# Graph sum layer: the own-row half of the mixing made in the stage that normalises, kept in DRAM with its bias, and a reordered score chain in attention

## The chip, the cores and the metric

The kernel runs on one core of one Trainium2 chip, as one launch. The metric is device time in microseconds (us) from start to end of an execution, the median of several runs. TensorE (PE), VectorE (DVE), ScalarE (ACT), GpSimd (POOL) and SyncE (SP) each run their own instruction stream in order and meet at semaphores.

## The reference

`x` is 6250 nodes by 256 features in float32, with 100000 edges sorted by target node. Four residual steps follow each other; the change touches the first (attention, three layers) and the third (graph sum):

```python
x = x + gat3(layernorm(x))                  # three attention layers, segment softmax over edges
x = x + moe_gelu(layernorm(x))              # 8 experts, 2 a node, and a shared one
e = layernorm(x)                            # "embeddings" of the graph sum
ego  = e @ W1.T + b1                        # own-row product
nb   = segment_sum(edge_val * e[src], dst)  # neighbours
side = (nb + nb * e) @ W2.T + b2
out  = leaky_relu(ego + side, 0.2)
x = x + out / max(norm(out), 1e-12)
x = x + moe_relu(layernorm(x))              # 4 experts, 2 a node, and a shared one
```

## The kernel before

Nodes lie in NT = 49 tiles of 128 rows; blocks of UT = 7 tiles make NB = 7 blocks. Edges lie in 28 groups (NG) of 28 columns (GB) of 128 edges. Code is written by hand for each engine; stages follow each other with a barrier between, so a stage's time is that of its latest engine, the last DMA that it waits for included. In combine and mix_end every loop over tiles is unrolled.

**attention_pass** (three times, line 872 on). POOL gathers the rows of a group's 28 columns by 28 indirect DMAs (L956) into one half of a two-half buffer. DVE waits for a group's rows, copies the scores to `terms` (L1085), and runs a chain of small operations, in turns with PE's transposes, which finds each edge's segment maximum: `differ` (L1027 to L1032, six operations that compare the open node tile's peak; ACT makes `scale` of them, L1151), `shut`, `x`, scans `up` and `top` (L1090 to L1096), `scale_sums` (L1038), after PE's `prow` the scans `fore` and `back` (L1103), `scale_old` (L1044), after PE's `pcar` the copy `carry` (L1109) and the scans again, `merge`, and after `paid` the weighing of the rows (`weigh`, L1058) with one-hot matrices (`hots`, L1064) for PE's sum over edges (L1217). `differ` waits for `kept`, ACT's copy of the last finished sum.

**combine** (line 2062 on) adds the expert outputs, `routed`, to X and normalises to `rows`/`emb`. SP loads the blocks of `routed` (896 KB each) into a ring of R = 3 (L2081), waiting only for `added`, so up to three blocks ahead. DVE runs `vary(i)` (add L2106, statistics) and `norm(i)` (L2121) in the order vary(0), vary(1), norm(0), vary(2), norm(1), ..., vary(6), norm(5), norm(6). ACT takes the square root of a block's variances and issues the store of each normalised block to the DRAM table `emb` (L2093). PE and POOL have nothing to do.

**loads** and **add_into** follow: SP loads the mixing weights `w` (W1T and W2T), two bias rows and the router's weights, and DVE adds the biases to `gbias`. Then **edge_pass** gathers rows of `emb` and sums them.

**mix_end** (line 1555 on), tile by tile: SP loads a block of `emb`; DVE makes `fin` = (1 + e) * nb (L1590); PE transposes e and fin (4 of 128x128, L1615); ACT copies them to `xt`; PE multiplies with W1T and W2T (4 products of 128x128 by 128x256, each float32 product is 2 recorded instructions, L1623); DVE adds `gbias` (L1598) and applies the leaky slope (L1600); ACT squares. In DVE's order tile t's `fin` stands ahead of tile t-2's last two operations; in PE's, tile t's transposes ahead of tile t-1's products.

Of the kernel before, what the change touches and what calls it, by code (L numbers as in the profile page):

```python
# [35 lines left out]
ALU = mybir.AluOpType  # L36
# [3 lines left out]
P = 128  # L40
# [831 lines left out]
def attention_pass(nc, kit, c, table, accs):  # L872
# [7 lines left out]
    with kit.stage() as st:  # L880
# [55 lines left out]
        with nc.Block() as block:  # L936
# [41 lines left out]
            def _(dve):  # L978
# [95 lines left out]
                with dve.Fori(0, NG // 2) as i:  # L1074
                    for h in range(2):
# [6 lines left out]
                        for k, n in enumerate((HALF, GB - HALF)):  # L1082
# [4 lines left out]

                        dve.wait_ge(kept, m + low + 2)
                        differ(before)
                        linked(v.tensor_copy(shut[:, :], flat(c.penT[:, 1, ds(m), :])))  # L1090
# [7 lines left out]

                        dve.wait_ge(scaled, m + 1)
                        scale_sums(before)  # L1100
                        dve.wait_ge(rowed, m + 1)
# [3 lines left out]
                                             ALU.add, ALU.max).then_inc(rkept, 1)  # L1105

                        scale_old()
                        dve.wait_ge(carried, m + 3)
# [446 lines left out]
def mix_end(nc, kit, c, acc, table, outs):  # L1555


    with kit.stage() as st:
        sb, ps, sem = st.sb, st.ps, st.sem
        fin = sb("fin", [P, UT, D])  # L1560
        xt = sb("xt", [P, UT, 4, P])
        pT = [ps(f"pT{k}", [P, 4, P]) for k in range(2)]
        pH = [ps(f"pH{k}", [P, D]) for k in range(2)]
# [3 lines left out]
        prod, hkept, made, squared = sem("prod"), sem("hkept"), sem("made"), sem("squared")  # L1567
        emb_in = sem("emb_in")

        with nc.Block() as block:  # L1570
            @block.sync
            def _(sp):
                for i in range(NB):
                    sp.dma_start(outs["sbuf"][:, i * UT:(i + 1) * UT, :],
                                 table[i * UT * P:(i + 1) * UT * P, :].rearrange("(k p) d -> p k d", p=P)
                                 ).then_inc(emb_in, 16)
                    sp.wait_ge(emb_in, (i + 1) * 16)

            @block.vector
            def _(dve):  # L1580
                v = nc.vector
                dve.sem_inc(hkept, UT)
                dve.sem_inc(made, UT)
                for t in range(NT + 2):
                    if t < NT:
                        k = t % UT
                        if not k:
                            dve.wait_ge(emb_in, (t // UT + 1) * 16)
                        dve.wait_ge(turned, t + 1)
                        v.scalar_tensor_tensor(out=fin[:, k, :], in0=outs["sbuf"][:, t, :], scalar=1.0,  # L1590
                                               in1=acc(slice(t, t + 1)).rearrange("p o d -> p (o d)"),
                                               op0=ALU.add, op1=ALU.mult).then_inc(fin_made, 1)
                    if t > 1:
                        m = t - 2
                        dve.wait_ge(prod, m + 1)
                        if m:
                            dve.wait_ge(made, UT + m)
                        v.tensor_tensor(junk[:, :], pH[m % 2][:, :], c.gbias[:, :], ALU.add).then_inc(hkept, 1)  # L1598
                        dve.wait_ge(hkept, UT + m + 1)
                        v.scalar_tensor_tensor(out=outs["sbuf"][:, m, :], in0=junk[:, :], scalar=SLOPE,  # L1600
                                               in1=junk[:, :], op0=ALU.mult, op1=ALU.max).then_inc(made, 1)

            @block.tensor
            def _(pe):
                pe.sem_inc(turned, UT)
                for t in range(NT + 1):
                    k = t % UT
                    if t < NT:
                        pe.wait_ge(fin_made, t + 1)
                        if t > 1:  # L1610
                            pe.wait_ge(kept, UT + t - 1)
                        for f in range(4):
                            from_ = outs["sbuf"][:, t, :] if f < 2 else fin[:, k, :]
                            at = f % 2 * P
                            ins = nc.tensor.transpose(pT[t % 2][:, f, :], from_[:, at:at + P], c.ident[:, :])  # L1615
                        ins.then_inc(turned, 1)
                    if t:
                        m = t - 1
                        pe.wait_ge(kept, UT + m + 1)
                        if m > 1:  # L1620
                            pe.wait_ge(hkept, UT + m - 1)
                        for f in range(4):
                            ins = nc.tensor.matmul(pH[m % 2][:, :], xt[:, m % UT, f, :], outs["w"][:, f, :],  # L1623
                                                   start=(f == 0), stop=(f == 3))
                        ins.then_inc(prod, 1)
# [172 lines left out]
def experts_gelu(nc, kit, c, a, rows, slot_i, gates, group_i, slots_in, X, hT, room):  # L1798
# [3 lines left out]
    with kit.stage() as st:  # L1802
# [6 lines left out]
        xt = sb("xt", [P, 2, GS])  # L1809
        ys = sb("ys", [P, 2, D])  # L1810
        SLOTS = (MAXG + 1) * 2
# [249 lines left out]

def combine(nc, kit, c, X, emb, table):


    R = 3
    with kit.stage() as st:
        sb, sem = st.sb, st.sem
        routed = sb("routed", [P, R, UT, D])
        stats = sb("stats", [P, UT, 6])
# [3 lines left out]
        own, added, varied, rooted = sem("own"), sem("added"), sem("varied"), sem("rooted")  # L2073
        normed, stored = sem("normed"), sem("stored")
        with nc.Block() as block:
            @block.sync
            def _(sp):
                for i in range(NB):
                    if i >= R:
# [3 lines left out]
                                 ).then_inc(loaded[i % R], 16)  # L2083

            @block.scalar
            def _(act):
                for i in range(NB):
                    act.wait_ge(varied, i + 2)
                    nc.scalar.activation(std[:, i % 2, :], mv[:, i % 2, :, 1], ACT.Sqrt, bias=eps[:, :]
                                         ).then_inc(rooted, 1)  # L2090

                    act.wait_ge(normed, (i + 1) * UT)
                    act.dma_start(table[i * UT * P:(i + 1) * UT * P, :].rearrange("(k p) d -> p k d", p=P),  # L2093
                                  emb[:, i * UT:(i + 1) * UT, :]).then_inc(stored, 16)
                act.wait_ge(stored, 16 * NB)

# [228 lines left out]
def program(nc, a, out):  # L2325
# [13 lines left out]
    c.slots_in = slots_in  # L2339
    c.slot_of = dram("slot_of", [(MAXG + 1) * GS, 2])  # L2340
    c.routed = dram("routed", [NP + P, D])
    table = [dram(f"table{k}", [NP, RW]) for k in range(2)]
    emb = dram("emb", [NP, D])

    with kit.stage() as whole:
# [37 lines left out]
        with kit.stage() as rest:  # L2383
            xT = rest.sb("xT", [P, 2, NP])
            gate = rest.sb("gate", [P, NT, E1])
            gw, gb = rest.sb("gw", [P, 2, E1]), rest.sb("gb", [P, 1, E1])
            with kit.stage() as st:

                with kit.stage() as moe:
# [5 lines left out]
                    wr = moe.sb("wr", [P, 2, E0])  # L2395
                    loads(nc, kit, [(wr[:, :, :], a["L0_ffn_Wr"].rearrange("(k p) e -> p k e", p=P))])
                    with kit.stage() as route:
# [7 lines left out]
                    experts_gelu(nc, kit, c, a, rows, slot_i, (w1, w2), group_i, slots_in, X, hT, xT[:, 1, :])  # L2405
                    combine(nc, kit, c, X, rows, emb)
                sumsq = st.sb("sumsq", [P, NT])
                w = st.sb("w", [P, 4, D])
                c.gbias = st.sb("gbias", [P, D])
                b = st.sb("b", [P, D])  # L2410
                loads(nc, kit, [
                    (w[:, 0:2, :], a["W1T"].rearrange("(k p) n -> p k n", p=P)),
                    (w[:, 2:4, :], a["W2T"].rearrange("(k p) n -> p k n", p=P)),
                    (c.gbias[:, :], a["L1_gnn_b1"].rearrange("(o n) -> o n", o=1).to_broadcast([P, D])),
                    (b[:, :], a["L1_gnn_b2"].rearrange("(o n) -> o n", o=1).to_broadcast([P, D])),
                    (gw[:, :, :], a["L1_ffn_gW"].rearrange("(k p) e -> p k e", p=P)),
                    (gb[:, 0, :], a["L1_ffn_gb"].rearrange("e o -> o e").to_broadcast([P, E1]))])
                add_into(nc, kit, c.gbias[:, :], b[:, :])

                sums = xT[:, :, :].rearrange("p k n -> p (k n)").rearrange("p (t d) -> p t d", d=D)  # L2420
# [10 lines left out]
            experts_relu(nc, kit, c, a, xT, gate, X, out)  # L2431


def add_into(nc, kit, to, ap):
    with kit.stage() as st:
        done = st.sem("done")
        with nc.Block() as block:
            @block.vector
            def _(dve):
                nc.vector.tensor_tensor(to, to, ap, ALU.add).then_inc(done, 1)  # L2440

# [50 lines left out]
```

## Time and profile before

| what | value |
|---|---|
| median of the runs | 6542.59 us |
| the profiled execution's own time | 6540.51 us |
| its span, first to last instruction | 6538.9 us |
| mean granted TensorE clock | 0.819 of 2.4 GHz |
| busy share: PE, POOL, DVE, ACT | 66%, 56%, 51%, 13% |

The profiled execution lies 2.1 us under the median; 1.6 us of it lie outside its span. No engine is busy all the way: the stages have different limits, and busy shares are averages over them.

### The profile page before, as it was taken

How to read it: one execution, taken by the hardware profiler on the slowest of the kernel's cores; microseconds unless marked ns; L12 is line 12 of the kernel's file. 1: busy time of each engine (PE TensorE's matmuls, PEld its weight loads, DVE VectorE, ACT ScalarE, POOL GpSimd, SP SyncE). 2: the span in 40 equal slices, each digit the busy share in tenths (PEclk: the TensorE clock that was granted, in tenths of full speed). 3: DMA queues.
4: the chain of work that ended last, by engine and by line, in shares of the span. 5: the costliest groups of instructions: out<-in, count | busy, mean ns of one | idle time of the engine just before them, and what ended most of it. 6: DMA issues, size and time to landing. Idle time of an engine off the chain costs nothing. (4 is left out here: it accounts for less than half of the span.)

```text
span 6538.9 us, 91130 instructions
## 1 busy us (share of the span) xinstructions
PE 4292.3 (66%) x16953; PEld 3195.3 (49%) x16954; DVE 3314.1 (51%) x7793; ACT 826.7 (13%) x2019; POOL 3662.1 (56%) x3758
## 2 busy tenths in 40 slices
PE   1455667644656665455667369999992556666879
PEld 1333444433434443333444258888882444444745
DVE  7355666665566666566666731111114444444655
ACT  0200000020000002000000123322220000000322
POOL 3577777657777764777777047222222777775000
PEclk9777778876778887677888569999996777888889
DMA  5443333334333333433333233133334333333011
GB/s 174 123 113 106 106 106 106 89 110 120 106 106 106 106 95 99 124 106 106 106 106 100 84 123 88 37 66 58 60 51 117 105 105 105 105 105 96 23 49 43
DMA packets 495005, 627.74 MB, mean 96 GB/s; under 512 B 260172, under 2 KB 376904, under 8 KB 493256
## 3 DMA queue, kind: packets, MB, share of 16 engines
q0 software_dynamic: 191568, 486.53, 27.8%
q1 hardware_dynamic: 293816, 132.89, 7.6%
q10 hardware_dynamic: 9552, 7.61, 0.4%
q14 instruction: 52, 0.43, 0.0%
q8 instruction: 17, 0.28, 0.0%
HBM read 531.35 MB, written 95.78 MB: 96 GB/s over the span
## 5 line engine op out<-in xcount | busy, mean ns | idle before, releaser
L956 POOL DMA_INDIRECT rows<-table,ix x2352 | 2259.3, 961 | 741.2 <-issue 682.6
L1217 PE MATMUL acc<-rows,hot 128*128 x5856 | 1621.5, 435 | 228.0 <-DVE hot L1064 174.6
L1217 PEld LDWEIGHTS acc<-rows,hot 128*128 128x128 f32 x5856 | 1164.5, 211 | 641.4 <-issue 425.2
L1263 POOL DMA_INDIRECT rows<-emb,ix x784 | 742.0, 946 | 320.7 <-issue 229.0
L1064 DVE TENSOR_TENSOR hot<-lanes,drel 128x256 f32<-128x256 f32 x1464 | 610.2, 422 | 572.2 <-PE acc L1217 569.6
L1385 PE MATMUL acc<-rows,hot 128*128 x1952 | 582.6, 461 | 321.4 <-DVE hot L1306 308.0
L1058 DVE TENSOR_TENSOR rows<-rows,pw 128x1024 f32<-128x1024 f32 x588 | 711.6, 1210 | 0.0
L1385 PEld LDWEIGHTS acc<-rows,hot 128*128 128x128 f32 x1952 | 430.9, 232 | 456.4 <-issue 381.2
L1955 PE MATMUL p<-xt,w 128*128 128x256 f32 x2496 | 554.4, 380 | 25.4 <-DVE xt L2011 25.4
L1966 PE MATMUL p<-w,xT 128*128 128x256 f32 x2496 | 551.4, 379 | 0.0
L1955 PEld LDWEIGHTS p<-xt,w 128*128 128x128 f32 x2496 | 476.2, 191 | 90.7 <-issue 25.5
L1966 PEld LDWEIGHTS p<-w,xT 128*128 128x128 f32 x2496 | 474.2, 190 | 64.5
L1887 POOL DMA_INDIRECT routed<-ys,to_row x106 | 165.6, 1563 | 553.6 <-DVE ys L2052 340.0
L1985 ACT ACTIVATE xT<-p,b 128x256 f32<-128x256 f32 x624 | 290.2, 473 | 575.1 <-PE p L1955 572.2
L1158 ACT ACTIVATE accs<-acc x228 | 89.0, 390 | 2063.6 <-PE acc L1220 2063.6
L1306 DVE TENSOR_TENSOR hot<-lanes,drel 128x256 f32<-128x256 f32 x488 | 200.4, 422 | 217.4 <-PE acc L1385 216.3
L457 POOL DMA_INDIRECT spread<-logit,first_edge x147 | 176.1, 1198 | 225.7 <-ACT logit L1536 154.1
L2011 DVE STREAM_TRANSPOSE xt<-xg 128x512 f32<-128x512 f32 x79 | 56.2, 711 | 462.4 <-PE p L1955 445.6
L1182 PE MATMUL pS<-ident,terms 128*112 128x128 f32 x84 | 30.7, 365 | 390.3 <-DVE terms L1085 373.0
L1085 DVE COPY terms<-rows 128x112 f32<-128x112 f32 x84 | 22.2, 264 | 454.4 <-DMA rows<-table,ix 373.2
L1300 DVE TENSOR_TENSOR rows<-rows,wps 128x1024 f32<-128x1024 f32 x196 | 237.4, 1211 | 6.7 <-DMA rows<-emb,ix 6.7
L1182 PEld LDWEIGHTS pS<-ident,terms 128*112 128x112 f32 x84 | 12.7, 151 | 403.8 <-issue 403.8
(405 smaller groups left out, 4372.9 us busy)
## 6 DMA issues: line engine op xcount, KB each, us to landing
rows<-table,ix POOLq DMA_INDIRECT x2352, 2.8
xg<-slots_in SPq DMA_DIRECT2D x632, 32.0 KB
table<-hs SPq DMA_DIRECT2D x147, 130.0 KB, 2.0
own_row<-table SPq DMA_DIRECT2D x21, 896.0 KB, 11.2
slots_in<-zsp SPq DMA_DIRECT2D x9, 1664.0 KB
xin<-in_x POOLq DMA_DIRECT2D x14, 896.0 KB, 5.7
rows<-emb,ix POOLq DMA_INDIRECT x784, 2.7
w<-in_W1all POOLq DMA_DIRECT2D x9, 1024.0 KB, 7.4
```

The lines of the kernel that those rows point to most:

```text
L457: return pool.indirect_dma_start(c.spread, bass.IndirectOffsetOnAxis(ap=c.first_edge[:, t:t + 1], axis=0), c.logit[:, t, H:2 * H], None, b ...
L956: pool.indirect_dma_start(rows[:, h * GB + k, 0:RW], None, table, bass.IndirectOffsetOnAxis(ap=ix[:, h, k:k + 1], axis=0)).then_inc(landed ...
L1058: v.tensor_tensor(r, r, w.to_broadcast([P, W, H, HD]), ALU.mult).then_inc(weighed, 1)
L1064: v.tensor_tensor(hot[j][:, :, :], lanes[:, :, :].to_broadcast([P, 2, P]), c.drel[:, ds(q * W + j * 2, 2)].rearrange("p (k o) -> p k o", o ...
L1217: ins = nc.tensor.matmul(A, hot[j][:, k, :], four[:, j * 2 + k, :], start=False, stop=False, skip_group_check=True)
L1263: pool.indirect_dma_start(rows[:, h * GB + k, 0:D], None, table, bass.IndirectOffsetOnAxis(ap=ix[:, h, k:k + 1], axis=0)).then_inc(landed[ ...
L1300: v.tensor_tensor(r, r, w.to_broadcast([P, W, D]), ALU.mult).then_inc(weighed, 1)
L1306: v.tensor_tensor(hot[j][:, :, :], lanes[:, :, :].to_broadcast([P, 2, P]), c.drel[:, ds(q * W + j * 2, 2)].rearrange("p (k o) -> p k o", o ...
L1385: ins = nc.tensor.matmul(A, hot[j][:, k, :], four[:, j * 2 + k, :], start=False, stop=False, skip_group_check=True)
L1955: ins = nc.tensor.matmul(p1[f % 4][:, :], w1[b][:, k, f * P:(f + 1) * P], xt[:, k, :], start=(k == 0), stop=(k == 1))
L1966: ins = nc.tensor.matmul(p2[t][:, :], hT[:, f, t * P:(t + 1) * P], w2[b][:, f, :], start=(f == 0), stop=(f == FT0 - 1))
L1985: nc.scalar.activation(hT[:, f, :], p1[f % 4][:, :], ACT.Gelu, bias=b1[b][:, f:f + 1]).then_inc(bent, 1)
```

## The change

In **combine**, SP first loads W1T and the two bias rows. As each tile is normalised, PE transposes it and multiplies it with W1T, ACT copies both the transposes and the product out of PSUM, POOL adds the joined bias and, per block, issues the store of the 896 KB of `ego` to a new DRAM tensor. The store of the normalised block moves from ACT's queue to SP's. The buffer of `routed` lies in `xT`, which is free then. In **mix_end** the 2 transposes of e and the 2 products with W1T go; SP loads each block of `ego` behind that of `emb`, and DVE adds `ego` where it added `gbias`. The stage that loaded the weights and the one that added the biases go; W2T and the router's weights are loaded in the `loads` ahead of the experts (3 DMAs more there). `ys` of the experts lies in a spare part of `xT`. In **attention_pass** DVE's chain is reordered, and a group's first `hots` is moved ahead of the wait for `paid`.

```diff
@@ combine
+        def store(eng, i):
+            eng.wait_ge(normed, (i + 1) * UT)
+            eng.dma_start(table[...], emb[:, i * UT:(i + 1) * UT, :]).then_inc(stored, 16)
             def _(sp):
+                sp.dma_start(w[:, :, :], a["W1T"].rearrange("(k p) n -> p k n", p=P)).then_inc(fetched, 16)
+                for k, name in enumerate(("L1_gnn_b1", "L1_gnn_b2")):
+                    sp.dma_start(bias[:, k, :], a[name]...to_broadcast([P, D])).then_inc(fetched, 16)
                 for i in range(NB):
                     if i >= R:
                         sp.wait_ge(added, i - R + 1)
                     sp.dma_start(routed[:, i % R, :, :], ...).then_inc(loaded[i % R], 16)
+                    if i:
+                        store(sp, i - 1)
+                store(sp, NB - 1)
+                sp.wait_ge(stored, 16 * NB)
+            def _(pe):
+                for t in range(NT + 1):
+                    if t < NT:
+                        pe.wait_ge(normed, t + 1)
+                        if t > 1:
+                            pe.wait_ge(kept, t - 1)
+                        for f in range(2):
+                            ins = nc.tensor.transpose(pT[t % 2][:, f, :], emb[:, t, f * P:(f + 1) * P], c.ident[:, :])
+                        ins.then_inc(turned, 1)
+                    if t:
+                        m = t - 1
+                        pe.wait_ge(kept, m + 1)
+                        if m > 1:
+                            pe.wait_ge(copied, m - 1)
+                        for f in range(2):
+                            ins = nc.tensor.matmul(pH[m % 2][:, :], xt[:, m % 2, f, :], w[:, f, :], ...)
+                        ins.then_inc(prod, 1)
+            def _(pool):
...
+                for t in range(NT):
+                    pool.wait_ge(copied, t + 1)
+                    nc.gpsimd.tensor_tensor(row, row, bias[:, 0, :], ALU.add).then_inc(egos, 1)
+                    if k == UT - 1:
+                        pool.wait_ge(egos, t + 1)
+                        pool.dma_start(c.ego[i * UT * P:(i + 1) * UT * P, :]..., ego[:, i % 2, :, :])
+                for k in range(2):
+                    pool.wait_ge(ego_out[k], (NB + 1 - k) // 2 * 16)
             def _(act):
+                def take(m):
+                    i = m // UT
+                    if not m % UT and i > 1:
+                        act.wait_ge(ego_out[i % 2], i // 2 * 16)
+                    act.wait_ge(prod, m + 1)
+                    nc.scalar.activation(ego[:, i % 2, m % UT, :], pH[m % 2][:, :], ACT.Copy).then_inc(copied, 1)
-                for i in range(NB):
-                    act.wait_ge(varied, i + 2)
-                    ... Sqrt ...
-                    act.wait_ge(normed, (i + 1) * UT)
-                    act.dma_start(table[...], emb[...]).then_inc(stored, 16)
+                root(0)
+                for i in range(NB):
+                    if i < NB - 1:
+                        root(i + 1)
+                    for t in range(i * UT, (i + 1) * UT):
+                        act.wait_ge(turned, t + 1)
+                        nc.scalar.activation(xt[:, t % 2, :, :], pT[t % 2][:, :, :], ACT.Copy).then_inc(kept, 1)
+                        if t:
+                            take(t - 1)
@@ mix_end
                     sp.dma_start(outs["sbuf"][...], table[...]).then_inc(emb_in, 16)
+                    if i > 1:
+                        sp.wait_ge(hkept, i * UT)
+                    sp.dma_start(ego[:, i % 2, :, :], c.ego[...]).then_inc(ego_in[i % 2], 16)
                     sp.wait_ge(emb_in, (i + 1) * 16)
...
-                        for f in range(4):
-                            from_ = outs["sbuf"][:, t, :] if f < 2 else fin[:, k, :]
+                        for f in range(2):
+                            ins = nc.tensor.transpose(pT[t % 2][:, f, :], fin[:, k, f * P:(f + 1) * P], c.ident[:, :])
...
-                        for f in range(4):
+                        for f in range(2):
                             ins = nc.tensor.matmul(pH[m % 2][:, :], xt[:, m % UT, f, :], outs["w"][:, f, :], ...)
@@ attention_pass
                         v.tensor_copy(old[:, :], flat(accs[:, ds(low), :])).then_inc(saved, 1)
+                        hots(m * GP + low)
                         dve.wait_ge(paid, m + 1)
...
                             if l:
                                 weigh(h, l)
-                            hots(m * GP + low + l)
+                                hots(m * GP + low + l)
```

SP in combine, before (`routed` is the load of a block, `emb` the store of one):

```order
L2081 DMA routed<-routed 128x7x256 x7
```

and now (the buffer of `routed` is a part of `xT`):

```order
L2100 DMA w<-in_W1T 128x2x256
L2102 DMA bias<-in_L_gnn_b 128x256 x2
L2107 DMA xT<-routed 128x7x256 x2
L2094 DMA emb<-rows 128x7x256
L2107 DMA xT<-routed 128x7x256
L2094 DMA emb<-rows 128x7x256
L2107 DMA xT<-routed 128x7x256
L2094 DMA emb<-rows 128x7x256
```

From the third load on, each load stands behind the store of the block two before it; the pair repeats to the end.

DVE in a group's chain of attention_pass, before:

```order
L1085 COPY terms<-rows 128x112
L1088 ISA
L1027 COPY both<-old 128x8
...
L1032 TENSOR_TENSOR gone<-gone,peak 128x8
L1090 ISA
L1090 COPY shut<-penT 112x128
...
L1096 SCALAR_TENSOR_TENSOR top<-shut,up 112x128
L1038 ISA
L1038 TENSOR_TENSOR accs<-accs,scale 128x256
...
L1104 SCALAR_TENSOR_TENSOR back<-run,prow 1x112
L1044 TENSOR_TENSOR old<-old,scale 128x256
```

and now:

```order
L1085 COPY terms<-rows 128x112
L1088 ISA
L1088 COPY shut<-penT 112x128
...
L1094 SCALAR_TENSOR_TENSOR top<-shut,up 112x128
L1097 ISA
L1027 COPY both<-old 128x8
...
L1032 TENSOR_TENSOR gone<-gone,peak 128x8
...
L1102 SCALAR_TENSOR_TENSOR back<-run,prow 1x112
L1038 ISA
L1038 TENSOR_TENSOR accs<-accs,scale 128x256
L1039 TENSOR_TENSOR accs<-accs,scale 128x4
L1044 TENSOR_TENSOR old<-old,scale 128x256
```

`differ` moved behind the first scans, and `scale_sums` behind `back`, where `scale_old` follows it.

## Rows read from the trace of the kernel before

**Rows 1.** Groups by line: busy us, mean ns of one, idle before and what ended it

```profile
L956 POOL DMA_INDIRECT rows<-table,ix x2352 | 2259.3, 961 | 741.2 <-issue 682.6 <-PE acc L1217 32.3 <-DVE ix L981 25.6
```

**Rows 2.** Source view of L1085: what ended DVE's idle time before it (us, times)

```profile
  DMA rows<-table,ix: 373.2, 66
```

**Rows 3.** Timeline, a late group of attention layer 1: start, us, engine

```profile
1257.95 0.30 DVE L1027 COPY both<-old 128x8 f32<-128x8 f32 x1 [3.29 <-ACT accs L1158]
...
1258.06 0.29 PE L1182 MATMUL pS<-ident,terms 128*112 128x128 f32 x1 [0.75 <-issue]
...
1259.14 1.28 ACT L1151 ACT_TABLE_LOAD   x1 [1.23 <-issue]
1259.49 0.29 DVE L1092 TENSOR_TENSOR x<-pS,dT 112x128 f32<-112x128 f32 x1 [0.23 <-DVE shut L1090]
...
1263.11 0.16 DVE L1109 COPY carry<-pcar 112x2 f32<-112x2 f32 x1
```

**Rows 4.** Windows: length, PE, PEld, DVE, ACT, POOL busy, PEclk, DMA share, GB/s

```profile
4952.00:5013.00 61.00, 0.00 (x0) 0.00 (x0) 52.81 (x162) 3.39 (x8) 0.00 (x0) 0.50 0.60 196
...
6031.00:6043.00 12.00, 4.98 (x20) 4.24 (x20) 1.22 (x4) 1.19 (x2) 0.00 (x0) 0.57 0.49 154
6043.00:6143.00 100.00, 100.00 (x557) 88.22 (x556) 54.90 (x140) 45.73 (x139) 0.00 (x0) 1.00 0.15 47
6150.00:6250.00 100.00, 61.22 (x294) 57.94 (x294) 74.27 (x369) 22.39 (x60) 0.00 (x0) 0.51 0.00 1
```

**Rows 5.** Timeline of combine, of the loads behind it and of edge_pass's start

```profile
4952.09 28.55 SPq L2081 DMA_DIRECT2D routed<-routed  x7
...
4970.52 0.40 ACTq L2093 DMA_DIRECT2D emb<-rows  x1
4970.52 2.02 DVE L2106 TENSOR_TENSOR accs<-accs,routed 128x1792 f32<-128x1792 f32 x1
...
4978.23 2.02 DVE L2106 TENSOR_TENSOR accs<-accs,routed 128x1792 f32<-128x1792 f32 x1
...
5012.52 0.37 ACTq L2093 DMA_DIRECT2D emb<-rows  x1
5018.19 0.38 SPq L2321 DMA_DIRECT2D w<-in_W1T  x1
...
5020.59 0.47 SPq L2321 DMA_DIRECT2D gb<-in_L_ffn_gb  x1
...
5025.67 0.26 DVE L1288 COPY ix<-idx 128x28 int32<-128x28 int32 x2 [0.65 <-PEq L140]
```

**Rows 6.** Source view of L2081: the seven loads of `routed`

```profile
DMA to landing us min/median/max: 5.3/5.6/9.3
```

**Rows 7.** The same for its third load alone, issued at 4953.1

```profile
DMA to landing us min/median/max: 9.3/9.3/9.3
```

**Rows 8.** Timeline of mix_end: its first tile, and one period later

```profile
6037.54 1.10 DVE L1590 SCALAR_TENSOR_TENSOR fin<-rows,xT 128x256 f32<-128x256 f32 x3 [7.00 <-DMA rows<-emb]
...
6038.02 0.69 PE L1615 MATMUL pT<-ident,rows 128*128 128x128 f32 x2 [9.30 <-DVE fin L1590]
...
6042.87 0.42 DVE L1598 TENSOR_TENSOR junk<-pH,gbias 128x256 f32<-128x256 f32 x1 [4.24 <-PE pH L1623]
...
6043.33 0.42 DVE L1600 SCALAR_TENSOR_TENSOR rows<-junk 128x256 f32<-128x256 f32 x1
6043.67 0.42 DVE L1590 SCALAR_TENSOR_TENSOR fin<-rows,xT 128x256 f32<-128x256 f32 x1
...
6045.04 0.42 DVE L1598 TENSOR_TENSOR junk<-pH,gbias 128x256 f32<-128x256 f32 x1 [0.94 <-PE pH L1623]
...
6045.27 1.89 PE L1623 MATMUL pH<-w,xt 128*128 128x256 f32 x8
```

**Rows 9.** Groups by line and form on POOL: one elementwise operation, one block DMA

```profile
L180 POOL TENSOR_SCALAR_AFFINE_SELECT ident<-ident 128x128 f32<-128x128 f32 x1 | 0.3, 282 | 0.1
...
L529 POOL DMA_DIRECT2D xin<-in_x x7 | 6.7, 956 | 174.3 <-issue 145.6 <-DVEq L583 28.7
```

More of the change, by code:

```diff
@@ L1097, in _ @@
                                              ).then_inc(ended, 1)
-                        dve.wait_ge(scaled, m + 1)
-                        scale_sums(before)
+                        dve.wait_ge(kept, m + low + 2)
+                        differ(before)
                         dve.wait_ge(rowed, m + 1)
@@ L1105, in _ @@
                                              ALU.add, ALU.max).then_inc(rkept, 1)
+                        dve.wait_ge(scaled, m + 1)
+                        scale_sums(before)
                         scale_old()
@@ L1560, in mix_end @@
         fin = sb("fin", [P, UT, D])
-        xt = sb("xt", [P, UT, 4, P])
-        pT = [ps(f"pT{k}", [P, 4, P]) for k in range(2)]
+        xt = sb("xt", [P, UT, 2, P])
+        ego = sb("ego", [P, 2, UT, D])
+        pT = [ps(f"pT{k}", [P, 2, P]) for k in range(2)]
         pH = [ps(f"pH{k}", [P, D]) for k in range(2)]
@@ L1567, in mix_end @@
         prod, hkept, made, squared = sem("prod"), sem("hkept"), sem("made"), sem("squared")
-        emb_in = sem("emb_in")
+        emb_in, ego_in = sem("emb_in"), [sem(f"ego_in{k}") for k in range(2)]
         with nc.Block() as block:
@@ L1576, in _ @@
                                  ).then_inc(emb_in, 16)
+                    if i > 1:
+                        sp.wait_ge(hkept, i * UT)
+                    sp.dma_start(ego[:, i % 2, :, :],
+                                 c.ego[i * UT * P:(i + 1) * UT * P, :].rearrange("(k p) d -> p k d", p=P)
+                                 ).then_inc(ego_in[i % 2], 16)
                     sp.wait_ge(emb_in, (i + 1) * 16)
@@ L1597, in _ @@
                             dve.wait_ge(made, UT + m)
-                        v.tensor_tensor(junk[:, :], pH[m % 2][:, :], c.gbias[:, :], ALU.add).then_inc(hkept, 1)
+                        if not m % UT:
+                            dve.wait_ge(ego_in[m // UT % 2], (m // UT // 2 + 1) * 16)
+                        v.tensor_tensor(junk[:, :], pH[m % 2][:, :], ego[:, m // UT % 2, m % UT, :], ALU.add
+                                        ).then_inc(hkept, 1)
                         dve.wait_ge(hkept, UT + m + 1)
@@ L1809, in experts_gelu @@
         xt = sb("xt", [P, 2, GS])
-        ys = sb("ys", [P, 2, D])
+        ys = room[:, 2048:2048 + 2 * D].rearrange("p (k d) -> p k d", d=D)
         SLOTS = (MAXG + 1) * 2
@@ L2059, in _, with combine @@
                 experts(dve, expert)
-def combine(nc, kit, c, X, emb, table):
+def combine(nc, kit, c, a, X, emb, table, room):
     R = 3
     with kit.stage() as st:
-        sb, sem = st.sb, st.sem
-        routed = sb("routed", [P, R, UT, D])
+        sb, ps, sem = st.sb, st.ps, st.sem
+        w = sb("w", [P, 2, D])
+        bias = sb("bias", [P, 2, D])
+        xt = sb("xt", [P, 2, 2, P])
+        ego = sb("ego", [P, 2, UT, D])
+        pT = [ps(f"pT{k}", [P, 2, P]) for k in range(2)]
+        pH = [ps(f"pH{k}", [P, D]) for k in range(2)]
+        fetched, joined, copied = sem("fetched"), sem("joined"), sem("copied")
+        turned, kept, prod, egos = sem("turned"), sem("kept"), sem("prod"), sem("egos")
+        ego_out = [st.pool_sem(f"ego_out{k}") for k in range(2)]
+        routed = room.rearrange("p (r k d) -> p r k d", r=R, d=D)
         stats = sb("stats", [P, UT, 6])
@@ L2083, in _, with root @@
                                  ).then_inc(loaded[i % R], 16)
+                    if i:
+                        store(sp, i - 1)
+                store(sp, NB - 1)
+                sp.wait_ge(stored, 16 * NB)
+            @block.tensor
+            def _(pe):
+                pe.wait_ge(fetched, 48)
+                for t in range(NT + 1):
[12 more added lines that the diff above has]
+                        for f in range(2):
+                            ins = nc.tensor.matmul(pH[m % 2][:, :], xt[:, m % 2, f, :], w[:, f, :],
+                                                   start=(f == 0), stop=(f == 1))
+                        ins.then_inc(prod, 1)
+            @block.gpsimd
+            def _(pool):
+                pool.wait_ge(fetched, 48)
+                nc.gpsimd.tensor_tensor(bias[:, 0, :], bias[:, 0, :], bias[:, 1, :], ALU.add).then_inc(joined, 1)
+                pool.wait_ge(joined, 1)
+                for t in range(NT):
+                    i, k = t // UT, t % UT
+                    pool.wait_ge(copied, t + 1)
+                    row = ego[:, i % 2, k, :]
+                    nc.gpsimd.tensor_tensor(row, row, bias[:, 0, :], ALU.add).then_inc(egos, 1)
+                    if k == UT - 1:
+                        pool.wait_ge(egos, t + 1)
+                        pool.dma_start(c.ego[i * UT * P:(i + 1) * UT * P, :].rearrange("(k p) d -> p k d", p=P),
+                                       ego[:, i % 2, :, :]).then_inc(ego_out[i % 2], 16)
+                for k in range(2):
+                    pool.wait_ge(ego_out[k], (NB + 1 - k) // 2 * 16)
             @block.scalar
             def _(act):
-                for i in range(NB):
+                def root(i):
                     act.wait_ge(varied, i + 2)
@@ L2340, in program @@
     c.slot_of = dram("slot_of", [(MAXG + 1) * GS, 2])
+    c.ego = dram("ego", [NP, D])
     c.routed = dram("routed", [NP + P, D])
@@ L2387, in program @@
             with kit.stage() as st:
+                w = st.sb("w", [P, 2, D])
                 with kit.stage() as moe:
@@ L2405, in program @@
                     experts_gelu(nc, kit, c, a, rows, slot_i, (w1, w2), group_i, slots_in, X, hT, xT[:, 1, :])
-                    combine(nc, kit, c, X, rows, emb)
+                    combine(nc, kit, c, a, X, rows, emb, xT[:, 0, 0:3 * UT * D])
                 sumsq = st.sb("sumsq", [P, NT])
[L2408 to L2418, printed above, removed]
                 sums = xT[:, :, :].rearrange("p k n -> p (k n)").rearrange("p (t d) -> p t d", d=D)
@@ L2431, in program @@
             experts_relu(nc, kit, c, a, xT, gate, X, out)
[L2434 to L2440, printed above, removed]
 def inverse_norms(nc, kit, s):
```

22 lines of the change are left out of this document (13 added, 9 removed).

## The prediction

> **What bounds the kernel now.** The page's totals say little here, so I read the stages that the change touches, one by one: first the groups by line for attention, then the windows and timelines of combine and mix_end.
>
> Attention, over half of the span, is paced by GpSimd: 2352 gathers of 961 ns, each followed by some 0.29 us of its own issue (682.6 / 2352), so 28 of them are 35.0 us a group, and it waited for PE and DVE only 32.3 and 25.6 us in all [rows 1]. DVE, on the other hand, waited for gathered rows ahead of 66 of the 84 groups, 373 us in all [rows 2]. A shorter chain on DVE buys nothing in those 66. The others are the last ones of each layer, where the nodes have few edges, a group touches more tiles, and DVE and PE need some 38 us for it; there the chain counts in full.
>
> Combine is paced by DVE: 52.8 of 61.0 us busy, PE and GpSimd at 0 [rows 4], and a block takes 4978.23 - 4970.52 = 7.71 us without a wait for a load [rows 5]. Mix_end is paced by PE: 100.00 of 100 us busy at a granted clock of 1.00 (2.4 GHz), DVE 54.9, ACT 45.7 [rows 4]; a tile takes 6045.04 - 6042.87 = 2.17 us, 106 us for 49 [rows 8].
>
> **Mix_end.** Half of PE's instructions go: 1.08 us a tile at the same clock. DVE still has its three operations, which start 0.46, 0.34 and some 0.37 us apart (6042.87, 6043.33, 6043.67 [rows 8]): 1.17 us at least. Neither is what I expect to bind, but a loop of waits over two tiles: fin(t+1) starts, PE's transposes begin 0.48 us later (6038.02 - 6037.54), then tile t's product, whose turn is behind them; the transposes and 4 product instructions are half of a 2.17 us period plus the drain of the last, 1.25 to 1.45 us; then L1598, 0.46 to L1600, 0.34 to fin(t+3). The sum is 2.55 to 2.75 us for two tiles, 1.28 to 1.38 for one; I take 1.35. 49 x (2.17 - 1.35) = **-40 us**; at DVE's floor of 1.17 it is -49. The loads of `ego` (one of 896 KB, some 2.5 us, a block) hide under 9.5 us of work a block; were they bare, the first would cost 2.5 us.
>
> **Combine, SP's queue.** This is the step that takes most of that back. Before, SP ran up to three blocks ahead, so the 5.3 to 5.6 us that a load takes [rows 6] were never waited for after the first. Now load(i+1) is behind store(i-1) in SP's order, the store waits for norm(i-1), and vary(i+1) is DVE's very next work. So for vary(2) to vary(6) the whole way from the end of norm(i-1) to a landed block lies open: the store's issue (0.4), the load's latency (5.3 when alone [rows 6]), and the store's data ahead of it in the same queue. What data ahead costs, the third load of before shows: 9.3 us where the first took 5.6, though it was issued 1.0 us after it [rows 5, 7], so (10.3 - 5.6) / 2 = 2.35 us a block. The wait is 5.7 us if the store doesn't delay the load, 7.7 if fully; I take 7.3, since loads on one queue land one after another here. 5 x 7.3 = **+36.5 us** (28 to 40). Three more issues ahead of the first load, at 0.48 each (5018.19 to 5020.59 for five), are **+1.5**.
>
> The Trainium skill ("DMA: Bandwidth & Descriptors", section "Issuing engines are not separate DMA queues") says that the engine which issues a DMA doesn't matter for its transfer and that more issuers only save issue time. By that alone the moved stores would cost 7 x 0.4 = 3 us instead of 36; the second rival is the result that this gives.
>
> **Combine, its end.** PE has 7 tiles x 1.08 = 7.6 us a block (15 at half clock) in a period that is now 15 us, and ACT, with two copies a tile, has less to do than PE (its copy and square took 45.7 us for 46 tiles in mix_end [rows 4]): both fit. But norm(5) and norm(6) follow each other, so 14 tiles stand in front of PE when DVE has 5.5 us left. PE has then been idle for some us and starts at the lower clock, as at mix_end's start (0.57 over 12 us [rows 4]); I take 4.4 us at 2.17 for 2 tiles and 12 x 1.08: 17.4 us. From the end of vary(6): 0.7 to the first normalised tile, 17.4, 0.2 drain, ACT 0.45, GpSimd's add, its DMA. The add is not in the trace; the nearest row is an elementwise operation on 128 columns of 282 ns [rows 9], so 0.28 to 0.56 for 256 columns, and I take 0.5. A store of a block by GpSimd I price like its block load, some 5.5 us from issue to landing. Sum 24.8, and 1.2 to the next stage: 26. Before, two norms (6.1) lay between vary(6) and the last store's issue, and 5.7 from there to the next stage (5018.19 - 5012.52 [rows 5]): 11.8. So **+14** (10 without the slow clock, 27 if all 14 tiles run at half). The adds of the earlier blocks fall mostly into DVE's new waits.
>
> The Trainium skill ("GPSIMD Engine Reference", section "Performance versus the Vector engine") calls GpSimd the wrong place for elementwise work, 4497 ns for 2048 columns; an estimate by that page is 0.56 us for 256, which moves the sum by 0.1. No run so far shows a GpSimd add here.
>
> **The loads.** Gone are the weights' stage and the biases' stage: 5025.67 - 5018.19 = **-7.5 us** [rows 5]; the barrier behind combine stays. The `loads` ahead of the experts gets 3 issues of 0.48 and later landings: **+2** (1.4 to 3).
>
> **Attention.** In the late groups `x` could start when `pS` is done: 1258.06 + 0.29 + 0.06 = 1258.41 instead of 1259.49, so 1.08 us earlier [rows 3]. `differ`, 1.1 us, now stands in the wait for `prow` and outlasts it by 0.15; both scalings stand ahead of `carry`, where there was room for one: 0.4 lost. `carry` comes 0.5 earlier. The first `hots` (0.75 us) ahead of `paid` delays the first product by 0.2, since the weighing is later by that much. Net -0.3 a group in layers 2 and 3. Layer 1 has an ACT table load of 1.28 us ahead of `scale` in each group [rows 3], which lay under the first scans. It now starts when `differ` ends, and `scale_sums` and with it `carry` wait for it: carry comes 0.55 later than before, +0.75 with `hots`. Some six late groups a layer: +4.5 - 2 x 1.8 = +0.9, taken as **+1** (-6 to +8). `ys` in `xT` moves no instruction and is priced at nothing.
>
> **Sum.** -40 + 36.5 + 1.5 + 14 - 7.5 + 2 + 1 = +7.5 us on the profiled execution's own 6540.5, so 6548; the median of the runs is 2.1 us above that execution, which gives **6550**. Its own range, from the ends above, is 6530 to 6572. A difference under 2% (131 us) is about what a measurement of this kernel can't tell from none.
>
> **The rivals.**
> First, slower: the halved work lets the TensorE clock fall. In mix_end PE would be busy 80% instead of 100%, and the stage right behind it, with PE busy 61%, ran at a granted clock of 0.51 (1.2 GHz) [rows 4]. At half clock the loop is 0.48 + 2.7 + 0.84 for two tiles, 2.0 a tile, or PE's own 2.17: mix_end saves nothing (+40 against the sum), and combine's end costs its 27 (+13): 6603. It decides if the clock stays at 1.2 GHz for most of mix_end. Against it: at that clock PE would be busy without a pause, and that is the state in which mix_end's clock rose. Chance 0.08.
> Second, faster: the loads don't wait, because each block lands within DVE's other work: 6550 - 36.5 + 2.5 for the moved issues = 6516. It decides if SP gets past its wait before norm(i-1) ends, which the order shown excludes as I read it. Chance 0.04. The Trainium skill's sentence on issuing engines, above, taken alone leads to this time.
> Third, the chain: if `differ` behind the scans makes DVE the limit in all 84 groups, 84 x 0.75 = 63 us: 6612. Against it is DVE's wait for rows, 373 / 66 = 5.7 us in the mean [rows 2], which would have to be gone first. Chance 0.03.
> Fourth, GpSimd's adds take the SBUF from DVE's work or are as slow as its gathers (0.95 us): under 10 us in 49 adds, within the range.
>
> **How the numbers follow.** Forecast 0.85, rivals 0.08, 0.04, 0.03. Range 6525 to 6580: the forecast's own range and a little of the near sides of rivals one and two. None reaches 131 us, so within 2% is 0.98, and 0.01 each is left for what I haven't seen.
>
> **What would show it.** In the changed profile: DVE in combine idle for about 7 us ahead of the add of `routed` of blocks 2 to 6, released by a DMA; GpSimd's last `ego` store landing some 19 us behind the last normalisation; the combine stage near 118 us instead of 66; mix_end's tile at 1.3 to 1.4 us with DVE waiting for PE; late attention groups of layer 1 with DVE waiting for ACT's `scale`. I am wrong if combine keeps its 7.7 us a block, or if mix_end stays at 2 us a tile.

## The result, and the profile after

The changed kernel took 6575.5 us (median), the kernel before 6542.5: ratio 1.0049, 95% interval 1.0027 to 1.0072. That is inside the predicted 6525 to 6580 and within 2%, but 25 us above the predicted 6550, and above the forecast's own range, which ended at 6572. By stages of the two profiled executions (each from one row of a timeline to the next: first index copy of attention, last `t<-logit`, first issue of a stage by SP):

| stage | before | after | change | predicted |
|---|---|---|---|---|
| attention, three layers | 3355.2 | 3360.0 | +4.8 | +1 |
| loads ahead of the experts | 2.6 | 5.1 | +2.5 | +2 |
| router and experts | 1239.2 | 1239.2 | 0 | 0 |
| combine to the edge stage's index copy | 73.6 | 131.5 | +57.9 | +44.5 |
| edge stage | 1006.6 | 1015.6 | +9.0 | not priced |
| mix_end | 116.6 | 74.7 | -41.9 | -40 |
| what stands ahead and behind | | | +2.3 | 0 |

Combine, the windows of the changed kernel (columns as in [rows 4]; mix_end's middle below):

```profile
4960.30:5091.80 131.50, 68.45 (x294) 55.25 (x294) 54.27 (x162) 37.53 (x106) 44.58 (x57) 0.76 0.47 151
...
6115.00:6175.00 60.00, 55.98 (x271) 39.41 (x270) 50.79 (x134) 37.52 (x132) 0.00 (x0) 0.98 0.58 183
```

DVE is busy for 54.3 us in combine, with the same 162 instructions that took 52.8 us before [rows 4], but the stage now lasts 131.5 us. The waits of DVE there (us, times, longest) say where it stood:

```profile
DVE accs L2190 <- DMA xT<-routed: 53.9, 6, 9.8
DVE ix L1289 <- PEq L140: 22.2, 1, 22.2
```

The first line is the wait for blocks: 9.64 us for the first one, and 44.3 us in five waits for blocks 2 to 6. The second is the stage's end. The timeline shows one such wait, and the end (GpSimd's adds between left out):

```profile
4981.80 1.04 DVE L2205 TENSOR_SCALAR rows<-accs,mv,rstd 128x256 f32<-128x256 f32 x3
4982.87 0.38 SPq L2094 DMA_DIRECT2D emb<-rows  x1
4983.29 0.56 SPq L2107 DMA_DIRECT2D xT<-routed  x1
...
4990.81 2.24 DVE L2190 TENSOR_TENSOR accs<-accs,xT 128x1792 f32<-128x1792 f32 x1 [7.97 <-DMA xT<-routed]
...
5057.88 0.72 POOL L2146 TENSOR_TENSOR ego<-ego,bias 128x256 f32<-128x256 f32 x1 [0.36 <-ACT ego L2166]
5058.62 2.03 DVE L2190 TENSOR_TENSOR accs<-accs,xT 128x1792 f32<-128x1792 f32 x1 [8.27 <-DMA xT<-routed]
5058.96 2.27 POOL L2146 TENSOR_TENSOR ego<-ego,bias 128x256 f32<-128x256 f32 x1 [0.36 <-ACT ego L2166]
...
5063.10 0.58 DVE L2196 BATCH_NORM_AGGREGATE mv<-stats 128x2 f32<-128x6 f32 x7
...
5084.93 0.94 POOL L2149 DMA_DIRECT2D ego<-ego  x1 [0.30 <-POOL ego L2146]
5091.80 0.26 DVE L1289 COPY ix<-idx 128x28 int32<-128x28 int32 x2 [22.20 <-PEq L140]
```

The last normalised tile ends at 4982.84, SP issues the store, then the load, and DVE stands until 4990.81. At the end the last statistics are done at 5063.68, the last `ego` store is issued 21.3 us later, and the edge stage starts after 28.1 us.

Mix_end's DVE, one period of two tiles:

```profile
6131.41 0.42 DVE L1607 TENSOR_TENSOR junk<-pH,ego 128x256 f32<-128x256 f32 x1 [0.27 <-PE pH L1631]
...
6134.02 0.42 DVE L1607 TENSOR_TENSOR junk<-pH,ego 128x256 f32<-128x256 f32 x1 [0.27 <-PE pH L1631]
```

6134.02 - 6131.41 = 2.61 us for two tiles, 1.31 a tile, at a granted clock of 0.98, where [rows 8] had 2.17.

What nobody had touched changed too: the edge stage's 784 gathers, before and after (after the bar: busy us, then the mean ns of one).

```profile
L1263 POOL DMA_INDIRECT rows<-emb,ix x784 | 742.0, 946 | 320.7 <-issue 229.0 <-DVE ix L1288 82.2 <-PE acc L1385 9.4
...
L1264 POOL DMA_INDIRECT rows<-emb,ix x784 | 751.0, 958 | 245.1 <-issue 229.3 <-PE acc L1386 9.1 <-DVE ix L1289 6.6
```

### The profile page after: what moved, and what is told of

It reads as the page before. It is cut to its first block and busy times, and to the rows that moved or that the text cites. A ratio compares the mean times of both kernels' runs of the same rounds, so it can differ in the third digit from the quotient of the medians.

```text
span 6573.5 us, 91404 instructions
## 1 busy us (share of the span) xinstructions
PE 4307.1 (66%) x16953; PEld 3193.6 (49%) x16954; DVE 3290.7 (50%) x7792; ACT 853.6 (13%) x2117; POOL 3734.6 (57%) x3815
## 5 line engine op out<-in xcount | busy, mean ns | idle before, releaser
L1895 POOL DMA_INDIRECT routed<-xT,to_row x106 | 165.7, 1563 | 553.6 <-DVE xT L2060 327.9
L1085 DVE COPY terms<-rows 128x112 f32<-128x112 f32 x84 | 22.3, 265 | 447.6 <-DMA rows<-table,ix 367.3
```

## The experiments

"Gathers" below are the edge stage's, by the mean of one, unless attention's are named.

**The kernel before once more.** Nothing edited.

> The kernel before, unchanged, profiled on the chip of this call. In the changed kernel every indirect gather of 128 rows takes about 11 ns more than in the profile of before (L1264: 957 against 946 ns in the mean field of the edges), which would make the 9 us that the edge stage lost. My theory: that belongs to the changed program (its new DRAM tensor moves the others, or its code), so this run shows 946 ns again and an edge stage of about 1006.6 us. Rival: it belongs to the chip or the run; then this run shows about 957 ns and an edge stage of about 1015 us.

Measured: 6546.5 us, gathers 946 ns, edge stage 1008.3 us. The slower gather belongs to the program.

**Loads ahead.** SP's order alone:

```
-                    if i:
-                        store(sp, i - 1)
-                store(sp, NB - 1)
+                    if i >= R:
+                        store(sp, i - R)
+                for i in range(NB - R, NB):
+                    store(sp, i)
```

> The changed kernel with one thing moved: SP issues a block's store only behind the load three blocks on, so that loads again run up to three blocks ahead of DVE. My theory: the 44.3 us that DVE waited for blocks 2 to 6 of combine (7.97, 9.11, 9.13, 9.82, 8.27) come from the place of the loads behind the stores in SP's order. They go, combine (from its first SP issue to the edge stage's index copy) goes from 131.5 to 85 to 95 us, since PE, ACT and GpSimd then have a block of 7 tiles (7.6 us of PE at the fast clock) in DVE's 7.7 us period and end later behind it; total 36 to 46 us under the changed kernel, about 6530 to 6540. First rival: DVE waited because PE's, ACT's and GpSimd's new traffic or the stores slow the loads themselves; then waits of 5 us a block or more stay and under 15 us are gained. Second rival: PE starts late and at the slow clock and is the bound of the stage, 49 tiles of 2.17 us are 106 us; then DVE's waits for loads go, the stage stays at 115 us or more and the gain is 10 to 16 us.

Measured: 6536.9 us, 38.7 under the changed kernel (0.9991 of before, interval 0.9982 to 1.0). Combine took 91.0 us, and of the waits for blocks only the first was left:

```profile
DVE ix L1289 <- PEq L140: 16.1, 1, 16.1
...
DVE accs L2191 <- DMA xT<-routed: 10.3, 1, 10.3
```

SP's order cost 40.5 us of combine; both rivals fall. The gathers stayed at 957 ns.

**Attention's order alone, and the rest alone.** The first is the kernel before with the `attention_pass` part of the change, the second the changed kernel without it.

> The kernel before with the change of attention's DVE order alone; mixing as before. My theory after the trace of the changed kernel: the 16 or so late groups gain 0.2 to 0.5 us each (the five of layer 1 took 185.83 instead of 186.88 us), the ACT table load of layer 1 doesn't wait for DVE, so the total is 3 to 8 us under before if the gathers keep their 946 ns. Rival, the prediction's: layer 1 loses 0.75 us a group, so the total is 0 to 8 us above before. If the gathers of the edge stage take 957 ns here, whatever makes them slower is in the attention edit or in the chip, not in the new DRAM tensor, and the total is some 10 us above that.

> The changed kernel with attention's DVE order as before; the mixing as changed. My theory: 3 to 8 us above the changed kernel, 6578 to 6584, gathers of the edge stage at 957 ns as in the changed kernel if the new DRAM tensor is what slows them. Rival (the prediction's layer 1 penalty): 0 to 8 us under the changed kernel. Gathers at 946 ns would say that the attention edit slows them, and the total would then be some 9 us lower.

Measured: 6533.9 us alone (0.9985 of before, interval 0.9976 to 0.9994), so -9.9 us; 6586.2 without it (1.0067 of before, interval 1.0055 to 1.008), 10.7 above the changed kernel. The gain is real, larger than I expected, and not where I looked for it. Attention alone, on GpSimd:

```profile
L956 POOL DMA_INDIRECT rows<-table,ix x2352 | 2249.6, 956 | 741.1 <-issue 684.1 <-PE acc L1218 30.5 <-DVE ix L981 25.6
```

Its gathers are busy 2259.3 - 2249.6 = 9.7 us less than in [rows 1], close to the whole gain, while their median stays at 946 ns. It is won where gathers set the pace: when the gathers of the 23rd group start, the three layers are 2.9, 2.4 and 4.5 us ahead of before, 9.8 of the 11.1 us by which the profiled attention stage is shorter. Counted in the timeline, 88 gathers took 1.05 us or more before and 53 do now (97 and 65 in the programs with the new mixing; over all runs here 88 to 97 in the old order, 46 to 68 in the new). 50 of the 88 lay beside DVE's `accs<-accs,old` and `accs<-peak`, L1051 and L1052, which came once in each group, and 49 beside the two copies that follow them, L1118 and L1120; in the new order 10 lie beside the first two. Which of DVE's operations holds a gather up no run separates. The gathers of the edge stage took 947 ns with the attention edit alone and 957 ns with the rest alone: the mixing edit slows them.

**Where the slower gathers come from.** Four programs. The new DRAM tensor declared last, in the kernel with loads ahead; and the kernel before with that tensor declared and unused:

```
-    c.ego = dram("ego", [NP, D])      # ahead of c.routed
     emb = dram("emb", [NP, D])
+    c.ego = dram("ego", [NP, D])
```

> The kernel with loads ahead (e2) and one line moved: the new DRAM tensor is declared after all others, so that the tables, the routed rows and the node embeddings keep the places in DRAM that they have in the kernel before. Gathers of the edge stage took 946 to 947 ns in the three programs without the mixing change and 957 to 958 ns in the three with it, on every chip tried. First theory: the slower gather comes from where the gathered tensors lie; then the edge stage's gathers are back at 946 ns, its 784 gain 9 us and attention some 14, and the total goes from 6537 to about 6513. Second theory: it comes from the program that GpSimd runs (its adds and its stores in combine); then gathers stay at 957 ns and the total at 6537.

> The kernel before with the new DRAM tensor declared at the same place as in the changed kernel, and never used. First theory (the place of the gathered tensors in DRAM): the gathers of the edge stage take 957 ns instead of 946, and the total is 20 to 25 us above before with no other instruction changed. Second theory (GpSimd's own program): 946 ns and the time of before.

Measured: 6537.9 us with 958 ns, and 6542.0 us with 947 ns. The tensor's place is not it. Then GpSimd's adds taken away, with loads ahead: the biases as a third product on TensorE, the stores still by GpSimd, or by ScalarE:

```
+    nc.tensor.matmul(pH[m % 2][:, :], c.ones[0:2, :], bias[:, :], start=False, stop=True)
-    nc.gpsimd.tensor_tensor(row, row, bias[:, 0, :], ALU.add).then_inc(egos, 1)
```

> The kernel with loads ahead (e2) with the biases added by TensorE (a third product instruction of two rows of ones by the two bias rows, into the same bank) instead of by GpSimd; GpSimd still issues the stores of the own-row product. Gathers: 957 ns if they are slowed by the tensor's place or by GpSimd's stores, 946 ns if by GpSimd's arithmetic. Combine: two of the four instruction halves of a tile's 1.085 us of PE are products, so a third of the same length makes 1.36 us a tile, more than DVE's 7.7 us for 7 tiles allows (1.10): 10 us more at the end of PE, 1 us less for the GpSimd add that ends the chain: combine 97 to 101 us against 91.0. Total 6543 to 6547 with gathers at 957 ns, 24 us less with 946. Rival: GpSimd's adds had been slowing DVE or the stores (one took 2.27 us beside DVE's add); then combine gets no longer.

> As the kernel with the biases added by TensorE (e6), and ScalarE issues the stores of the own-row product, so that GpSimd runs in combine nothing, as before. Gathers: 946 ns if GpSimd's stores or adds slow them, by code or by their queue; 957 ns if it is the place of the tensors in DRAM. Combine: within 2 us of the kernel with TensorE's bias. Total as that one's if the gathers are the same, 24 us less if they go back.

Measured: 947 ns in both, so it is GpSimd's arithmetic and not its stores. The line of the program in which GpSimd only stores:

```profile
L1264 POOL DMA_INDIRECT rows<-emb,ix x784 | 742.4, 947 | 245.0 <-issue 228.8 <-PE acc L1386 9.8 <-DVE ix L1289 6.5
```

But the totals were 6619.4 and 6618.4 us, far above what I expected. Combine took 196.4 us instead of 97 to 101:

```profile
4980.00:5020.00 40.00, 40.00 (x94) 23.28 (x94) 15.21 (x49) 9.59 (x26) 2.03 (x2) 0.50 0.37 124
```

TensorE was busy without a pause and the granted clock stayed at 0.50 (1.2 GHz) to the end of the stage, a tile 3.47 us. One of the nine executions of the first program took 6543.9 us, 72 us or more under the other eight (6616.1 to 6627.3); it has no trace. So the same product was tried with 128 rows, 126 of them zero:

```
-        bias = sb("bias", [2, D])           ...  c.ones[0:2, :], bias[:, :]
+        bias = sb("bias", [P, D])           ...  c.ones[:, :], bias[:, :]
```

> As the kernel with the biases added by TensorE (e6), in which the granted clock stayed at 0.50 through the whole of combine although PE was busy without a pause (a tile 3.47 us), but with the bias product made of 128 rows, 126 of them zero, instead of 2. Theory: the product of 2 rows is what kept the clock down; then the clock rises in combine as with loads ahead, a tile takes 1.6 to 1.75 us once it is up, PE is the bound, and combine takes 100 to 115 us. Rival: a third product a tile, of whatever rows, or PE's long queue keeps it down; then the clock is 0.50 again and combine lasts some 180 us. Gathers 947 ns in either case.

Measured, in a single execution: 6525.1 us, combine 103.0 us, a tile 1.52 us, gathers 948 ns:

```profile
4980.00:5020.00 40.00, 40.00 (x213) 34.59 (x212) 25.09 (x75) 17.88 (x57) 2.88 (x3) 1.00 0.59 206
```

The clock rose with the rows of that product as the only change on TensorE, so the two-row product is the likely reason why it stayed down. It isn't shown to hold it down every time: 12 of the 13 executions of the two programs with two rows took 6616 us or more, one took 6543.9, and the program with 128 rows ran once.

**One add, early.** The kernel before with a single GpSimd add of zeros in its first stage:

```
+    nc.gpsimd.tensor_tensor(c.ident[:, :], c.ident[:, :], c.ident[:, :], ALU.add).then_inc(zeroed, 1)
```

> The kernel before with a single GpSimd tensor-tensor add more, of a 128x128 tile of zeros to itself in the very first stage, long before any gather that is compared. My theory after the runs without GpSimd arithmetic (edge gathers 947 ns) and with it (957 to 958 ns), in which the tensor's place in DRAM made no difference: a program that holds such an add makes all indirect gathers of GpSimd about 11 ns longer, wherever the add stands. Then edge gathers take 957 ns here, the edge stage 1015 us instead of 1007, attention some 15 us more, and the total is 20 to 26 us above before, 6564 to 6569. Rival: it is the adds of combine as such (their number, their code between the stages); then one add at the start changes nothing and the time is that of before.

Measured: 6558.4 us (1.0022 of before, interval 1.0013 to 1.0032), +15.2 us for one instruction. My theory held for half of it: attention's gathers went from a median of 946 to 953 ns, but the edge stage's stayed at 947:

```profile
L958 POOL DMA_INDIRECT rows<-table,ix x2352 | 2272.9, 966 | 741.5 <-issue 686.3 <-PE acc L1219 29.0 <-DVE ix L983 25.7
L1265 POOL DMA_INDIRECT rows<-emb,ix x784 | 742.1, 947 | 320.5 <-issue 228.8 <-DVE ix L1290 82.0 <-PE acc L1387 9.7
```

So the effect isn't one of the whole program, and it ends somewhere between the experts' gathers (977 ns here, 961 to 966 without the add) and the edge stage. In the changed kernel the adds stand behind attention and attention's gathers are slow all the same; what carries that over no run shows. More GpSimd code alone doesn't do it, since the programs in which GpSimd only issues stores in combine have 946 to 948 ns; but no run puts another GpSimd operation in the add's place.

**A better version.** Loads ahead, the biases added by VectorE, a block at a time, three buffers, and no arithmetic on GpSimd:

```
+    v.tensor_tensor(rows, rows, bias[:, 0:1, :].to_broadcast([P, UT if k is None else 1, D]), ALU.add).then_inc(egos, 1)
```

> The kernel with loads ahead (e2) with the biases added by VectorE, a block of 7 tiles at a time in place (the last block tile by tile), three buffers for the own-row product; GpSimd only stores. Gathers: 947 ns, so about 23 us less than with loads ahead. Combine: DVE has 6 block adds of 2.0 us and 7 tile adds of 0.35 more, 14 us, of which some 4 fall into its wait for PE at the end: combine 99 to 103 us against 91.0. Total 6522 to 6528. Rival: the gathers stay at 957 ns as GpSimd still issues the stores; then 6545 to 6550.

Measured: 6516.6 us, 0.9959 of before (interval 0.9945 to 0.9972), 59 us under the changed kernel; attention's order alone gives 9.9 of the 26.5 us under before. In the profiled execution, the shortest of the five with 6505.4 us, gathers took 946 ns and combine 89.9 us: DVE's adds took 15.1 us, and its wait at the end fell from 16.1 us to 7.2.

```profile
DVE ix L1289 <- PEq L140: 7.2, 1, 7.2
```

I had expected 99 to 103 us for combine, and missed what GpSimd's adds did to DVE. With loads ahead and GpSimd adding, DVE was busy for 63.3 us:

```profile
4961.73:5052.73 91.00, 57.48 (x294) 47.28 (x294) 63.31 (x163) 36.27 (x106) 47.62 (x57) 0.82 0.65 218
```

Here it was busy for 68.0 us, and 68.0 - 15.1 = 52.9 without its own adds. So about 10 us of DVE's time in the run with loads ahead went to standing beside GpSimd's adds. In the changed kernel (54.3 us) most of these adds fell into DVE's waits for loads.

## Why the prediction came out as it did

- **The total, inside the range in part by luck.** 6575.5 us lies above the forecast's own 6530 to 6572; it is inside 6525 to 6580 by the margin taken from the first rival, which did not come. And 10 us that the prediction did not see, gained in attention, hide part of a cost that it did not see either: without the attention part the kernel took 6586.2 us, outside the range. The prediction's remark that less than 2% can't be told from none is too wide: one GpSimd add gave 1.0022 with an interval of 1.0013 to 1.0032.
- **Mix_end, right.** Predicted 1.35 us a tile and -40 us, measured 1.31 and -41.9. The loop of waits is what paces it: 0.48 us from `fin` to PE's transposes, 1.34 to L1607, 0.46 to L1610 and 0.34 to the next `fin` but one (6129.59, 6130.07, 6131.41, 6131.87, 6132.21) are the 2.62 us of two tiles. The clock stayed up, with PE busy 93% (55.98 of 60 us) where the first rival had 80%, so that rival did not come here.
- **SP's queue, right in mechanism, too small.** Predicted 36.5 us, measured 44.3 (7.97 to 9.82 a wait where I took 7.3, and even my fully delayed case was 7.7). A landed block took 4990.81 - 4983.29 = 7.5 us behind its issue, where 7.3 less the store's issue of 0.4 left 6.9; in that wait only the store of `emb` ran beside it. In the other four GpSimd issued an `ego` store 1.6 us behind the load, and the block landed after 7.7 to 9.3 us; the prediction had no `ego` store there, and no run separates its share. The first load cost 9.64 us of waiting instead of 5.5, +4.1 against +1.5: it was issued 1.4 us later, as priced, but landed after 8.3 us instead of 5.6, behind the weights and biases in the same queue, whose transfer was priced at nothing. The run with loads ahead gives 40.5 us back. The sentence of the Trainium skill ("DMA: Bandwidth & Descriptors", section "Issuing engines are not separate DMA queues"), that issuing from several engines saves only the time of issuing, is not contradicted: SP still issues those stores there. What cost the time was the order of waits on one engine, which that sentence doesn't speak of.
- **Combine's end, right.** Predicted +14; 28.1 instead of 11.8 us behind the last statistics is +16.3. A GpSimd add took 0.72 us where I took 0.5. (The lower end of 10 is a slip: without the slow clock the prediction's own terms give 12.)
- **Attention, wrong in mechanism.** I priced a shorter chain in late groups at -0.3 each and a penalty of layer 1 behind the ACT table load, +1 in all. The penalty doesn't exist: the table load ran while DVE's `differ` was still to come, and only the activation behind it waits, as a late group of layer 1 in the changed kernel shows:

```profile
1263.43 1.28 ACT L1152 ACT_TABLE_LOAD   x1 [1.22 <-issue]
...
1265.48 0.18 ACT L1152 ACTIVATE scale<-gone 128x8 f32<-128x8 f32 x1 [0.76 <-DVE gone L1032]
```

[rows 3] could have told: there, too, the idle time ahead of the load is "issue", so it waited for nothing that the profile shows. A late group gained 4.76 - 4.30 = 0.46 us from `pS` to `carry`. But most of the edit's -10 us, outside my -6 to +8, comes from fewer long gathers, which I had not looked for.
- **GpSimd's adds, the step that failed.** The fourth rival put their cost at under 10 us and only in combine; the sum had nothing for them outside it. The gathers of the stages around them each took 11 ns more: +9.0 us in the edge stage, and +14.9 in attention, which took 3370.1 us with the adds and the old order against 3355.2 before. These 24 us, hidden in part by attention's gain, and the 13 us that combine took beyond its terms make the miss.

The sum by measured terms: -41.9 + 57.9 + 2.5 + 9.0 + 14.9 - 10.1 + 2.3 = +34.6 us, the difference of the two profiled executions. It is the table's rows, with attention's +4.8 split by the run in the old order, so it adds up by construction.

## What to carry to other kernels

When a store is moved to another engine's queue, look at what its wait now stands in front of: here the loads of the next blocks, worth more than the matrix work that was saved. Half of a TensorE-bound stage was worth having (loads ahead still took 6536.9 us, attention's order alone 6533.9) only once its other half ran under an engine that was busy anyway, without a load stall and without a helper on the engine that paces other stages. After a change compare the durations of instructions that were not touched; a nanosecond matters when there are 3000 of them.

## What the runs showed of the hardware

- A program with a GpSimd tensor-tensor add has longer GpSimd gathers, those ahead of the add included: attention's median went from 946 to 953 ns with one add at the start and to 957 ns with 50 adds in combine, the edge stage's from 946 to 957 ns with the 50 and not at all with the one. The gathers' own code, data and lists were the same. Why is open.
- A GpSimd add of 128x256 took 0.72 us alone and 2.27 us beside DVE's two-input add: begun 0.34 us behind it, it ended 0.58 us behind it (5061.23 and 5060.65). The Trainium skill ("SBUF — State Buffer", section "SBUF: two separate sides") says of a DVE instruction with two SBUF inputs and a GpSimd one that reads SBUF that whichever starts first holds the port pair that they share for the whole instruction, and the other waits. This row agrees, but for 0.14 us.
- It goes the other way too: a DVE normalisation of 128x256, 0.41 us in the median, took up to 2.24 us in the run with loads ahead, where GpSimd added beside it, and at most 0.67 us where GpSimd did no arithmetic (the better version).
- TensorE, busy without a pause from its first tile on, was granted 0.50 (1.2 GHz) through a stage of 196 us when every third product had 2 rows, and 1.00 (2.4 GHz) in the same window with 128 rows. One profiled execution of each program shows this; of the executions with 2 rows that have no trace, one took 72 us less than the others.
